# Output projection in three rounded products instead of one float32 product

## The reference

```
q, k, v = (cproj(Wq), cproj(Wk), cproj(Wv))       # complex, 16 heads of 64
...                                               # rotation, distance, decay, log1p, causal mask
A = jax.nn.softmax(logits, axis=-1)
out = jnp.einsum('bhij,bjhd->bihd', A.astype(v.dtype), v)
y = jnp.concatenate([out.real.reshape(B_, N_, DKt), out.imag.reshape(B_, N_, DKt)], axis=-1)
return y @ Wo                                     # (2 * 1024) x 256
```

## Time and profile before

| | us |
|---|---|
| median of the runs | 1877.73 |
| the profiled execution | 1878.49 |
| its span | 1876.7 |
| PE busy | 1792.1 (95%) |
| DVE busy | 1628.9 (87%) |
| ACT busy | 1580.4 (84%) |
| POOL busy | 1469.7 (78%) |

### The profile page before, as it was taken

One profiled execution on the slowest core, in us unless ns is written; L12 is line 12 of the kernel. 1 busy time (PEld: TensorE's weight loads), 2 busy tenths in 40 slices (PEclk: granted clock), 3 DMA queues, 4 the chain that ended last, 5 costly groups with the idle time before them and its releaser, 6 DMA issues.

```text
span 1876.7 us, 35392 instructions
## 1 busy us (share of the span) xinstructions
PE 1792.1 (95%) x10672; PEld 1476.5 (79%) x10672; DVE 1628.9 (87%) x3848; ACT 1580.4 (84%) x3259; POOL 1469.7 (78%) x1291
## 2 busy tenths in 40 slices
PE   4799999999999999999999999999999999988996
PEld 3577788878888888778888888788888888867886
DVE  7799989988988889888888999888988988895884
ACT  5798889898888889898988888988988888885563
POOL 5677888878888888888888888788888888862663
PEclk8899999999999999999999999999999999998998
DMA  6311211131112211131213011221112111200111
GB/s 187 114 68 46 85 46 68 46 102 46 63 52 90 64 49 44 45 124 46 68 46 99 32 63 52 82 89 49 46 42 91 46 46 46 68 13 12 46 47 44
DMA packets 61085, 117.77 MB, mean 63 GB/s; under 512 B 13489, under 2 KB 42929, under 8 KB 52705
## 3 DMA queue, kind: packets, MB, share of 16 engines
q1 hardware_dynamic: 60512, 115.51, 18.3%
q10 hardware_dynamic: 384, 0.00, 0.0%
HBM read 99.64 MB, written 21.36 MB: 64 GB/s over the span
## 4 chain that ended last, share of the span: by engine, by line
PE 72%; DVE 10%; ACT 4%; issue 3%; POOL 1%; DVEq 0%; POOLq 0%; ACTq 0%
PE pa L759 15%; PE py L823 13%; PE ps L799 12%; PE po L834 10%; PE pp L789 8%; PE pp L811 6%; PE pa L770 4%; PE pa L778 2%; DVE lg L1603 2%; DVE stats L1630 1%; DVE rm L1472 1%; DVE acc L1652 1%; DVE tabs L1690 1%; DVE lg L1596 1%; POOL rstd L602 1%
## 5 line engine op out<-in xcount | busy, mean ns | idle before, releaser
L583 POOL TENSOR_TENSOR qk<-rm 64x512 f32<-64x512 f32 x504 | 697.2, 1383 | 93.2 <-PE ps L799 49.1
L593 POOL TENSOR_TENSOR ek<-tabs,kn 128x512 f32<-128x512 f32 (+3 forms) x512 | 463.8, 912 | 126.4 <-DVE lg L1596 99.4
L1603 DVE CUSTOM_DVE_ANT_0 lg<-lg,tabs,ncog 128x512 f32<-128x512 f32 (+3 forms) x512 | 446.7, 890 | 0.0
L759 PE MATMUL pa<-xt,wt 128*128 128x512 f32 x1488 | 421.9, 419 | 4.4 <-DVE rm L1478 2.7
L1472 DVE TENSOR_TENSOR rm<-pa,tabs 128x512 f32<-128x512 f32 x504 | 327.2, 677 | 74.1 <-POOL qk L583 66.1
L799 PE MATMUL ps<-qk 128*128 128x512 f32 (+3 forms) x1024 | 366.5, 442 | 7.8 <-DVE lg L1596 7.6
L823 PE MATMUL py<-pt,vt 128*128 128x128 f32 x2560 | 348.5, 275 | 0.1
L1596 DVE CUSTOM_DVE_ANT_0 lg<-ps,ek,qb 128x512 f32<-128x512 f32 (+3 forms) x512 | 279.3, 546 | 79.3 <-issue 61.1
L823 PEld LDWEIGHTS py<-pt,vt 128*128 128x128 f32 x2560 | 331.7, 192 | 16.2 <-issue 0.3
L759 PEld LDWEIGHTS pa<-xt,wt 128*128 128x128 f32 x1488 | 274.0, 191 | 56.9 <-issue 6.2
L1169 ACT ACTIVATE lg<-lg,qb 128x512 f32<-128x512 f32 (+3 forms) x512 | 273.0, 557 | 14.4 <-DVE lg L1596 10.4
(11 more groups left out here) (187 smaller groups left out, 2242.5 us busy)
## 6 DMA issues: line engine op xcount, KB each, us to landing
xt<-xs_d SPq DMA_DIRECT2D x56, 1024.0 KB, 4.8
tabs<-vec_d SPq DMA_DIRECT2D x7, 1536.0 KB, 6.5
xs_d<-xt SPq DMA_DIRECT2D x6, 1024.0 KB, 4.0
wt<-wraw_d SPq DMA_DIRECT2D x7, 768.0 KB, 6.6
acc<-in_L_attn_x SPq DMA_DIRECT2D x8, 512.0 KB, 6.1
tabs<-in_L_attn_x SPq DMA_DIRECT2D x8, 512.0 KB, 5.4
out<-tabs SPq DMA_DIRECT2D x8, 512.0 KB, 3.2
tabs<-rope_d SPq DMA_DIRECT2D x56, 64.0 KB, 5.9
```

The lines of the kernel that those rows point to most:

```text
L583: pool.tensor_tensor(qk[part * DH:(part + 1) * DH, z * HH + hh, :], rm[row, 2 * part, :], rm[row, 2 * part + 1, :], ALU.add if part else A ...
L593: pool.tensor_tensor(ek[:, n % 2, 0:w], tab(par, hh, E2_T, w), kn[:, hh, 0:w], ALU.mult).then_inc(ek_pool, 1)
L759: last = mm(pa[r][:, :], wproj(par, z, kt, a, r * P, (r + 1) * P), xbuf[x][:, kt, b, :], start=(n == 0), stop=(n == 3 * KT - 1))
L1603: dve.tensor_tensor_reduce(lg[:, hh, at(n)], lg[:, hh, at(n)], tab(par, hh, T3_T, w), ncog[:, par, 0, hh:hh + 1], 3e38, ALU.add, ALU.min, ...
```

## The change

The output weights and y are split into high and low parts, as x is. wot now holds the high and low parts of one group (the even groups); the odd groups' weights go to the first half of hx. They are first copied to a scratch tensor in DRAM and loaded from there with one transfer; ACT makes the high part and POOL the low part, in the iteration that opens the group. yt holds the high and low parts of one head at a time: ACT writes the high part (keep_y), DVE subtracts it from py (keep_low, new). out_project runs three rounded products instead of one float32 product and waits for DVE's part (y_dve) instead of ACT's. attend of head 1 waits for DVE too, since keep_low still reads py. keep_y of head 1 waits for the end of head 0's projection.

Three places of the order change. On PE, attend(cp, 1, 0) moves behind out_project(cp, 0, 0), and out_project(cp, 0, 1) moves from behind attend(cp, 1, 3) to between the two halves of values. On ACT, keep_turned(cp, 1, 2) moves behind log(c, 1, 0). On DVE, keep_low(0) stands behind distance(c, 1, 1), keep_low(1) behind the last rotate.

```
+
+        def out_views(par):
+
+            return [(wot, hx)[par][:, a, :] for a in range(2)]
+
+        def high_output_weights(act, g):
+            act.wait_ge(wo_in[g % 2], 16 * (g // 2 + 1))
+            hi, lo = out_views(g % 2)
+            act.activation(hi, lo.bitcast(F32), ACT.Copy).then_inc(wo_hi, 1)
+
+        def low_output_weights(pool, g):
+            pool.wait_ge(wo_hi, g + 1)
+            hi, lo = out_views(g % 2)
+            pool.tensor_tensor(lo, lo.bitcast(F32), hi.bitcast(F32), ALU.subtract).then_inc(wo_lo, 1)
...
-            def load_output_weights(g):
+            def copy_output_weights(g):
                 for c in range(2):
                     o = c * DK + g * HH * DH
-                    sp.dma_start(wot[c * DH:(c + 1) * DH, g % 2, :].rearrange("d (h n) -> d h n", h=HH),
-                                 wo_d[o:o + HH * DH, :].rearrange("(h d) n -> d h n", h=HH)).then_inc(wo_in[g % 2], 16)
+                    sp.dma_start(woraw_d[g, c * DH:(c + 1) * DH, :].rearrange("d (h n) -> d h n", h=HH),
+                                 wo_d[o:o + HH * DH, :].rearrange("(h d) n -> d h n", h=HH)).then_inc(wo_copy[g % 2], 16)
+
+            def load_output_weights(g):
+                sp.wait_ge(wo_copy[g % 2], 32 * (g // 2 + 1))
+                sp.dma_start(out_views(g % 2)[1].bitcast(F32), woraw_d[g]).then_inc(wo_in[g % 2], 16)
...
-                if j == (1 if g else 2) and g < G - 1:
+                if j == (1 if g else 6) and g < G - 1:
                     load_output_weights(g + 1)
...
+                if it.out is not None:
+                    low_output_weights(pool, it.out)
...
-                    pe.wait_ge(y_act, c[2] + hh)
+                    pe.wait_ge(y_dve, c[2] + hh)
...
-                    pe.wait_ge(y_act, c[2] + hh + 1)
+                    pe.wait_ge(y_dve, c[2] + hh + 1)
-                    last = mm(po[:, jj * D:(jj + 1) * D], yt[:, hh, j * P:(j + 1) * P], wot[:, par, hh * D:(hh + 1) * D],
-                              start=True, stop=True)
+                    for n, (a, b) in enumerate(PARTS):
+                        last = mm(po[:, jj * D:(jj + 1) * D], yt[:, a, j * P:(j + 1) * P], out_views(par)[b][:, hh * D:(hh + 1) * D],
+                                  start=(n == 0), stop=(n == 2))
                 last.then_inc(o_rdy, 1)
...
                     turn(cp, 1, 1)
                     turn(cp, 1, 2)
-                    attend(cp, 1, 0, 1 - it.slot)
                 scores(c, 1, 2)
                 if old:
                     turn(cp, 1, 3)
@@ -940,7 +967,10 @@
                 if it.own is not None and it.own < B - 1:
                     pe.wait_ge(x_lo, 2 * it.own + 4)
                 if old:
+                    if it.b_before == 0:
+                        pe.wait_ge(wo_lo, (it.t - 1) // B + 1)
                     out_project(cp, it.before, 0, 0)
+                    attend(cp, 1, 0, 1 - it.slot)
                 if nxt:
                     project(cn, it.behind, 1 - it.slot, it.xn, half, it.own, 1, 1)
                 if it.own == 1:
@@ -952,10 +982,11 @@
                     attend(cp, 1, 1, 1 - it.slot)
                     attend(cp, 1, 2, 1 - it.slot)
                 values(c, it.par, it.x, 0)
+                if old:
+                    out_project(cp, it.before, 0, 1)
                 values(c, it.par, it.x, 1)
                 if old:
                     attend(cp, 1, 3, 1 - it.slot)
-                    out_project(cp, it.before, 0, 1)
                 turn(c, 0, 0)
                 if not nxt:
                     f_transposes(0)
@@ -1010,7 +1041,6 @@
...
-                act.wait_ge(o_rdy, c[4] + 2 * hh + 2 - 4)
-                act.activation(yt[:, hh, :], py[:, :], ACT.Copy).then_inc(y_act, 1)
+                act.wait_ge(o_rdy, c[4] + 2 * hh)
+                act.activation(yt[:, 0, :], py[:, :], ACT.Copy).then_inc(y_act, 1)
...
+                log(c, 1, 0, it.slot)
                 if old:
                     keep_turned(cp, 1, 2)
-                log(c, 1, 0, it.slot)
...
+            def keep_low(c, hh):
+
+                dve.wait_ge(y_act, c[2] + hh + 1)
+                tt(yt[:, 1, :], py[:, :], yt[:, 0, :].bitcast(F32), ALU.subtract).then_inc(y_dve, 1)
+
...
+                if old:
+                    keep_low(cp, 0)
...
+                    keep_low(cp, 1)
                     add_output(cp, it.b_before, it.over, 0, 1)
```

More of the change, by code:

```diff
@@ L26 @@
 ACT = mybir.ActivationFunctionType
-It = namedtuple("It", "t half b par slot before behind b_before opens split own x xn over rope")
+It = namedtuple("It", "t half b par slot before behind b_before opens split own x xn over rope out")
 Rope = namedtuple("Rope", "turns ang sp sn om om2")
@@ L82, in build @@
         nco_d = scratch("nco_d", (H, 3))
+        woraw_d = scratch("woraw_d", (G, P, HH * D))
         acc = sb("acc", [P, B, NT, D])
@@ L87, in build @@
         wt = sb("wt", [P, 2, 3 * KT * 2 * W2], F32R)
-        wot = sb("wot", [P, 2, HH * D])
+        wot = sb("wot", [P, 2, HH * D], F32R)
         xt = [sb(f"xt{i}", [P, KT, 2, N], F32R) for i in range(2)]
@@ L98, in build @@
         vt = sb("vt", [P, 2, NT, HH * P])
-        yt = sb("yt", [P, HH, N])
+        yt = sb("yt", [P, 2, N], F32R)
         hx = sb("hx", [P, 4, N], F32R)
@@ L145, in rope_tiles @@
             return Rope(t0[0], t0[1], t0[2], sn, om[:, 2 * q:2 * q + 1], om[:, 2 * q + 1:2 * q + 2])
-        own_rope = rope_tiles((yt[:, 0, :], yt[:, 1, :], None), None, ROPES)
-        first_rope = rope_tiles((yt[:, 0, :], tabs[1][:, 6, :], tabs[1][:, 7, :]), pt[:, 1, :], 0)
+        own_rope = rope_tiles((sq[:, 1, 0, :], sq[:, 1, 1, :], None), None, ROPES)
+        first_rope = rope_tiles((flat(vt[:, 1, 2:NT, :]), tabs[1][:, 6, :], tabs[1][:, 7, :]), pt[:, 1, :], 0)
         ropes = [first_rope] + [rope_tiles((tabs[0][:, 0, :], tabs[0][:, 1, :], tabs[0][:, 2, :]), tabs[0][:, 3, :], k)
@@ L238, in build @@
         y_act = sem("y_act")
+        y_dve = sem("y_dve")
+        wo_copy = [sem(f"wo_copy{i}") for i in range(2)]
+        wo_hi = sem("wo_hi")
+        wo_lo = sem("wo_lo")
         mul_dve = sem("mul_dve")
@@ L302, in run_iterations @@
                         own=t + 1 if t + 1 < B else None, x=t % XBUF if g == 0 else t % 2,
-                        xn=(t + 1) % XBUF if t + 1 < B else (t + 1) % 2, over=t <= B, rope=rope))
+                        xn=(t + 1) % XBUF if t + 1 < B else (t + 1) % 2, over=t <= B, rope=rope, out=0 if t == 0 else g + 1 if j == B - 1 and g < G - 1 else None))
         def following(c):
@@ L459, in _ @@
             first_tables(0, 2)
+            copy_output_weights(0)
             load_output_weights(0)
@@ L495, in _ @@
                     copy_weights(1)
+                    copy_output_weights(1)
                 g, j = divmod(t, B)
@@ L506, in _ @@
                     copy_weights(g + 2)
+                    copy_output_weights(g + 2)
                 if j == 4 and g in (1, 3, 5):
@@ L900, in body @@
                     pe.wait_ge(w_lo, 3 * KT * (it.opens + 1))
-                    pe.wait_ge(wo_in[it.behind], 32 * (it.opens // 2 + 1))
                 if nxt:
@@ L1012, in _ @@
             pe.wait_ge(w_lo, 3 * KT)
-            pe.wait_ge(wo_in[0], 32)
             run_iterations(body)
@@ L1250, in body @@
                     high_weights(act, g, q)
+                if it.out is not None:
+                    high_output_weights(act, it.out)
                 if it.own == 1:
@@ L1396, in _ @@
         def _(dve):
-            credit(dve, (mul_dve, 8), (qb_dve, 1), (t_dve, 8), (x_dve, 8), (f_dve, 8), (rd_dve, 2), (acc_dve, 4))
+            credit(dve, (mul_dve, 8), (qb_dve, 1), (t_dve, 8), (x_dve, 8), (f_dve, 8), (rd_dve, 2), (acc_dve, 4), (y_dve, 2))
             tt, ts, stt, rec = dve.tensor_tensor, dve.tensor_scalar, dve.scalar_tensor_tensor, dve.reciprocal
@@ L1812, in _ @@
             split_low(0)
+            keep_low(c, 0)
             residual(1)
@@ L1817, in _ @@
             add_output(c, B - 1, False, 0, 1)
+            keep_low(c, 1)
             hidden(0, 0)
```

## The result

The changed kernel takes 1994.2 us (median of 4 runs, 1990.4 to 1994.9) against 1877.6 us before: 1.062 times as long, with a 95% interval of 1.061 to 1.064. The forecast was 1946 us with a range up to 1990: the direction was right, 48 us of 117 were missing, and the time lies 4 us outside the range.

A forecast was written before the change was run, and what follows sets the result against it. PE's matmuls set the pace at 25.1 us; two new waits on DVE make the period 26.2. 1878.5 + 68 (62 iterations) + 4 (weights) + 2 (tail) = 1952, stated as 1946 us, range 1890 to 1990.

The forecast's parts named there:

- What bounds the kernel: Steady iterations: an unbroken string of PE matmuls sets the pace, 25.1 us per iteration, with little room on DVE.
- What the matmuls give: Output projection: three rounded products save 0.12 us per pair, 0.48 per iteration, 30 us over 62 if PE stays the bound.
- First new wait: Head 0's projection waits for keep_low behind distance(1,1): 13.4 us from q-norm, PE waits about 0.9, period 25.57.
- Second new wait: Head 1: keep_y, keep_low, add_output after attend(1,3) take 2.27 us; PE waits 0.65 before projection (1,0); period 26.2.
- the port: Rival: keep_low pushes logits(0,2) or (0,3) onto POOL's rotation; 0.5 us more, period 26.7, 1983 us; 14%.
- keep their place: Argument against PE staying the bound: POOL's instructions near DVE's logits are released by the same DVE chain.
- the rival's counter-argument: DVE's 1.27 us pause behind logits(0,2) and (0,3) absorbs most of their blocking by POOL's rotation.
- waits that might ease: Releases were all set late and the q-norm anchor may ease by 0.1 us, 6 us over the run: 1952 becomes 1946.
- something that it counted nowhere: A lower granted clock in the steady part, then 1.00, was named but given no time in the sum.
- Small parts: Weight splitting 0.6 us per opening iteration, 4 us together; tail 2 us; queues and loads nothing or a few us.
- PE stays the bound: Rival: DVE's chain gives way as POOL moves aside, both waits vanish or hide, matmul saving stands: 1848 us; 12%.
- Only the first wait decides: Rival: keep_y(1) or add_output(0,1) come earlier than thought, period 25.57, 1913 us; 22%.

The follow-up runs named there:

- e7: Kernel before, float32 product kept, with only the change's new order on PE and ACT: 1922.5 us, ratio 1.025.
- e6: Kernel before with three rounded products, no subtraction of y, old order, and POOL's decay_norm(1,1) held behind logits(0,0): 1859.8 us, ratio 0.991.
- e4: Changed kernel without head 0's keep_low; that head's three products use the high part: 1961.0 us, ratio 1.045 to the kernel before.
- e5: Changed kernel without head 1's keep_low; that head's three products use the high part: 1961.0 us, ratio 1.045 to the kernel before.
- e12: Changed kernel with POOL's decay_norm(1,1) held behind logits(0,0) and logits(1,1) moved behind DVE's last rotations: 1943.2 us, ratio 1.036 to the kernel before.
- e2: Kernel before with three rounded products and split weights, no subtraction of y, two y slots, old order: 1875.9 us, ratio 0.9995.
- e3a: Complete changed kernel plus one wait: POOL's decay_norm(1,1) starts only behind logits(0,0): 1942.8 us, ratio 1.036 to the kernel before.

## Why the prediction was right or wrong

**What bounds the kernel, right.** PE at 25.10 us in most iterations behind the first seven, and DVE's section from the q-norm to distance(1,1) close behind. e7 shows how close: taking 0.89 us of PE's work from ahead of that point costs 0.66. The forecast missed that ACT's exponential, which the last transpose waits for, is as close; in the change itself DVE is later and decides.

**What the matmuls give, right.** 0.12 per pair, 0.48 per iteration; e6 measures 0.44, or 17 us in all with what the weights cost.

**First new wait, right in size.** Forecast 13.4 us from q-norm to projection, measured 13.34 in the iterations with a piece. One correction by e4 and e7: of what the iteration loses here only 0.37 us is the subtraction; the larger part comes with the new order (0.66 in e7, where PE's rows put it behind the place that attend(1,0) left).

**Second new wait, right.** Forecast 0.65; PE's rows have 0.55 ahead of projection (1,0) and 0.17 ahead of the k-norm, e5 measures 0.59 for the subtraction, and e12 rules out the rotations as its cause. Period forecast 26.2, measured 26.42 where there is a piece of weights; this 0.2 is 14 us over 62 iterations, and what makes it up was not followed.

**The step that failed: the port, taken as a rival with 14% and sized at nothing in the sum.** (The port stands for the two engines' hold on each other: DVE's logits and POOL's instructions.) The forecast took DVE's section with the blocking that the trace before had, and wrote that POOL's instructions "keep their place" because DVE releases them. One of them is not released by DVE: POOL's sum of squares waits for ACT (944.00 in POOL's rows above, idle 0.39) and ACT for PE's projection, and what stands behind it follows. The three rounded products ahead of that projection are shorter than the float32 product, so all of this comes 0.16 us earlier, which is more than DVE's lead of 0.11. That this is the cause is shown from two sides: e2 has the cheaper product with the old order and no keep_low, and POOL comes at 8.80 us behind qb as in the change; e7 has the new order with the float32 product, and POOL comes at 8.96 as before. e3a shows that the order of the two starts is what costs.

The price: 1.03 us in each of 13 iterations, 13 us, and in the seven that open a group, where POOL's new subtraction brings the same block on, 1.2 us with the weights' own work, for which the forecast had 0.6: 4 us more. Together 17 us, the largest part of the 48 that were missing. Without the 13 alone the time would be 1981 us, inside the range. The rest: 14 us are the 0.2 in the period; 6 us the forecast had taken off its sum (1952 to 1946) for waits that might ease; 5 us are the lower clock in three opening iterations, which the forecast had named as something that it counted nowhere; and some 3 us the first seven iterations, which grew by 12.6 us and not by seven times the 1.32 of the others. Why the clock fell in these three and not in the other four is not known; PE's waits ahead of it, 1.18 and 0.32 us, are the same in both.

The blocked logits(0,3), which the rival did name, is there in nearly every iteration (1138 ns on average), and as the rival's counter-argument said, the pause behind it takes it up: DVE still waits 0.17 us for ACT ahead of the second rotation behind it (956.17). e3a moves POOL out of the way and gives 51 us: 1942.8, within 4 us of the forecast of 1946. Part of that nearness is luck: the wait also frees logits(0,1), whose blocking the forecast had rightly kept.

The rule of the Trainium skill ("SBUF — State Buffer", section "SBUF: two separate sides") that whichever starts first holds the shared pair for its whole length fits these rows: 0.04 and 0.05 us decide over 0.8. keep_low, with one tile and one PSUM bank, stays at 685 ns, and the logits do not. The prediction used it for one place, logits(0,3), where the block did no harm; the same rule held for logits(0,0), and there it was the loss.

**Small parts.** The weights: forecast 0.6 us per group. With the one wait on POOL the opening iterations take 26.89 against 26.08, so 0.8. In the change itself four of them take 27.62, and three 29.2 with the lower clock.

**The rivals.** PE stays the bound: no. Only the first wait decides: no, e5 takes the second subtraction away and gains 0.59. The time fell near where the port case (1983) put it, 11 us above, but for a different logits than the one it named: that is luck, not a hit.

## What to carry to other kernels

When two engines block each other for whole instructions, as DVE's logits and POOL's instructions do here, the cost of each meeting depends on who arrives first, and 0.05 us can be worth 1 us per iteration: list every pair of such instructions on the stretch that is in the chain, not only the one next to the edit, and ask for each what releases the other engine and whether the change moves that. A wait that puts the idle engine behind the busy one is a cheap test and here a cheap cure. A saving is a change of time too: the cheaper product itself moved POOL forward by 0.16 us. And work taken from ahead of a wait is not neutral: the new order cost more (0.66) than the first subtraction, which made it necessary (0.37).

## What the runs showed of the hardware

- A logits instruction (two tiles read) of 512 columns takes 0.73 us if it starts 0.26 us ahead of POOL's instruction and 1.50 if it starts 0.05 us behind; both engines' rows are above. POOL pays as well: its instruction of 128x384 takes 1.01 us if it comes first, 1.34 if it starts 0.26 us behind DVE's logits and 1.50 if 0.11 us behind.
- A product of 128x256 in the rounded format takes 0.12 us in a row of 24, with a change of stationary data for each; three of them, 0.36, are 0.07 us faster than one float32 product of that size (0.43), and this showed as 0.44 us per iteration of eight.
- A saving on one engine can turn to a loss on another: in e2 the iterations are 0.45 us shorter than before where DVE comes first at the port, and 0.53 us longer where POOL came 0.04 us earlier than DVE.
- TensorE's granted clock fell to the lower of its two levels in three iterations of the steady part, right behind PE's waits of 1.18 and 0.32 us for DVE, and cost 1.6 us each time; four other iterations with the same waits kept the higher level.
